# ViT layer on one core: narrower stationary operands in the attention scores, and the maximum of the last three steps subtracted on VectorE

## The chip, the cores and the metric

The kernel runs on one core of a Trainium2 chip. The metric is the device time of one execution in microseconds. A core has TensorE (PE, matmuls out of SBUF into PSUM), VectorE (DVE), ScalarE (ACT), GpSimd (POOL, which here works on SBUF alone) and SyncE (SP, which issues the DMAs). Each engine runs its own list of instructions in order, and the lists meet at semaphores.

## The reference

One vision-transformer layer on 16 images of 96x96x3. Patches of 16x16 give 36 tokens per image and a width of 192:

```
h = patchify(x) @ W + b                                  # 16 x 36 x 192
q, k, v = split(h @ w_qkv.T)                             # 12 heads of 64
q = q * rsqrt(norm(q over heads) + eps); k likewise
scores = softmax(q @ k.T / scale[head])                  # per image and head: 36 x 36
h = layernorm(h + (scores @ v) @ w_out.T + b_out)
h = layernorm(h + ffn(h))                                # 8 experts, the best 2 per token
```

The FFN is a clamped gated one with sigmoid GELU. All data are fp32.

## The kernel before, in words

The 16 images are taken two at a time, in NU = 8 attention steps u = 0 to 7. The two images of a step, 36 tokens each, lie in PSUM lanes 0 to 35 and 64 to 99, so that LANES = 100. The 12 heads lie side by side, 36 columns each, six in one bank and six in the next. A step's bank pair is `s_bank(u) = 2 * (u % 2)`.

What a step u consists of, with the engine that does it:

- `scores(u)` (TensorE, L1488): 24 matmuls of q against k, in quarters of the array (64 rows by 64 columns), shown as 48 records since the data are fp32. The moving operand has 36 columns. The stationary one has 36 columns for the second image and 64 for the first; the 28 lanes more give lanes 36 to 63 defined values.
- `row_max(u)` (VectorE, L1020): the negated maximum of each row and head.
- `subtract_max(u)` (TensorE, L1500): two matmuls of a 100x100 identity against the broadcast maxima, which add the negated maximum to the scores in PSUM.
- `exps(u)` (ScalarE, L721): exponential from PSUM into the probabilities buffer u % 3 in SBUF.
- `row_sum(u)` and `row_recip(u)` (VectorE, L1027, L1034), then `probs(u)` (GpSimd, L525), which multiplies by the reciprocals.
- `p_transpose(u)` (TensorE, L1513), `pt_evac(u)` (ScalarE), `weighted(u)` (TensorE, L1530, probabilities times v, in quarters of the array too), `o_evac(u)` (ScalarE).

`project(g)` (TensorE, L1547 and L1550) multiplies a tile of about 108 tokens by the output weights and adds the residual, in one PSUM bank that all g share. Then the first layer norm: `ln1_stats(g)` (VectorE, L1039 to L1043, three instructions), `root(g)` (GpSimd, L531), `ln1(g)` (VectorE, L1057 and L1059). `project(g + 1)` waits for `ln1(g)`, since it writes the same bank. `h1_transpose(g)` (TensorE, L1559) and the router's `logits(g)` follow. From about 70 us on the experts' matmuls fill TensorE.

The order on each engine is written out by hand. TensorE, for k = 2 to 6: subtract_max(k), scores(k+1), weighted(k-2), p_transpose(k-1), with half of a v projection at k = 2, 3 and project(k-4) at k = 4, 5. Then subtract_max(7), h1_transpose(0), project(2), h1_transpose(1), weighted(5), p_transpose(6), logits(0), logits(1), h1_transpose(2).

VectorE, for k = 2 to 7: ln1_stats(k-5) at k = 5, 6; row_sum(k); ln1(0) at k = 5; row_max(k+1); ln1(1) at k = 6; row_recip(k); q_norm(k+3) at k = 2, 3, 4 (L976, the query's norm of a later step).

GpSimd, for k = 0 to 7: root(1) at k = 6; w_lo(7), w_lo(9), w_lo(10) at k = 3, 5, 6 (the low parts of later weights, L482, or L460 and L467); probs(k); at k = 4 then w_lo(8) and root(0); k_norm(k+3) (L518) while there is one. The low parts of q, k and weight data exist because large matmuls are made of several fp32r ones.

Waits that matter: `exps(u)` waits for subtract_max(u) and for p_transpose(u-3), which frees the probabilities buffer; `scores(u)` waits for exps(u-2), which frees the bank pair, and for the norms; `h1_transpose(0)` and `(1)` wait for exps(6) and exps(7), whose banks they write.

Of the kernel before, what the change touches and what calls it, by code (L numbers as in the profile page):

```python
# [10 lines left out]
B, SEQ = 16, 36  # L11
# [3 lines left out]
NP = H // 2  # L15
# [3 lines left out]
NU = B // 2  # L19
ST = 2 * SEQ  # L20
FST = 2 * ST
LANES = 64 + SEQ
# [13 lines left out]
def head_of(b, i, r):  # L36

    return 4 * i + (2 * r if b == 0 else 3 - 2 * r)
# [10 lines left out]
LAST_LO = 2 * NT - 1  # L49
NACT = 6  # L50
IN_PSUM = 3
XW = T + 2 * 128
STG = 6
NAT = 3
# [5 lines left out]
def vit_layer(nc, xw_in, w_qkv_a, w_qkv_b, w_out, w_gu_a, w_gu_b, w_down, small, out):  # L60
    f32, f32r, bf16, u32 = mybir.dt.float32, mybir.dt.float32r, mybir.dt.bfloat16, mybir.dt.uint32
    ALU = mybir.AluOpType
    ACT = mybir.ActivationFunctionType
# [3 lines left out]
    with ctx:  # L67
        def sb(name, shape, dt=f32):
            return ctx.enter_context(nc.sbuf_tensor(name, shape, dt))
# [4 lines left out]
        def f(ap):  # L74
            return ap.bitcast(f32)
# [7 lines left out]
        reg_r = sb("reg_r", [128, 4608 + 2 * NACT * TM + 3 * T], f32r)  # L83
        xw = reg_r[:, 0:NC * 2 * XW].rearrange("p (c k n) -> p c k n", c=NC, k=2)
        wd = reg_r[:, 0:NT * 384].rearrange("p (c n) -> p c n", c=NT)
# [4 lines left out]
        stage = sb("stage", [128, STG, STGW])  # L90
        reg_x = sb("reg_x", [128, NC * XW])
        xs = reg_x[:, :].rearrange("p (c n) -> p c n", c=NC)
# [4 lines left out]
        qk = reg_q[:, :].rearrange("p (m n) -> p m n", m=2 * NP)  # L97
# [45 lines left out]
        mx_r = sb("mx_r", [128, 2, H], f32r)  # L143
# [21 lines left out]
        ps = ctx.enter_context(nc.psum_tensor("ps", [128, 8, BANK], f32))  # L165
# [7 lines left out]
        def probabilities(u):  # L173

            return (Pr[:, 0], Pr[:, 1], Pr2)[u % 3]

        def slots_of(u, rows):

            return probabilities(u)[rows, :].rearrange("p (h j) -> p h j", h=H)[:, :, 0:SEQ]
# [93 lines left out]
        def lo_done(k):  # L273

            return (s_wlod, k + 1) if k < 2 else (s_wlop, w_count(k))
# [28 lines left out]
        def s_bank(u):  # L304
            return 2 * (u % 2)
# [9 lines left out]
        def spread_count(n):  # L315

            return (32 if n % 3 == 2 else 16) * (2 if n >= NT + IN_PSUM else 1)

# [28 lines left out]
        def pair_of(n):  # L347
            return pair(place(n))
# [7 lines left out]
        def gate_of(n):  # L356

            w = TS[n // NT]
            return ps[:, pair_of(n)[0], 0:w] if n >= IN_PSUM else glu[:, n, 0:w]

        def up_of(n):

            w = TS[n // NT]
            return ps[:, pair_of(n)[1], 0:w] if n >= IN_PSUM else upw[:, n, 0:w]

# [14 lines left out]
        def _(sp):  # L380
            sp.dma_start(xs[:, 0, 0:WX + TH], xw_in[0, :, 0:WX + TH]).then_inc(s_x[0], 16)
            sp.dma_start(xs[:, 0, WX + TH:XW], xw_in[0, :, WX + TH:XW]).then_inc(s_xb, 16)
            for c in range(1, NC):
# [21 lines left out]
            def spread(b):  # L405
# [4 lines left out]
                else:  # L410
                    sp.wait_ge(*lo_done(16))
                    for c in range(IN_PSUM, NT):
                        sp.wait_ge(s_spr[c], spread_count(c))
# [170 lines left out]
        def _(act):  # L584
# [130 lines left out]
            def exps(u):  # L715

                act.wait_ge(s_sub, u + 1)
                if u >= 3:
                    act.wait_ge(s_pt, u - 2)
                b = s_bank(u)  # L720
                nc.scalar.activation(slots_of(u, slice(0, LANES)).rearrange("p (b h) j -> p b h j", b=2),  # L721
                                     ps[0:LANES, b:b + 2, 0:6 * SEQ].rearrange("p b (h j) -> p b h j", h=6),
                                     ACT.Exp).then_inc(s_e, 1)
# [181 lines left out]
        def _(dve):  # L905
# [108 lines left out]
            def row_max(u):  # L1014

                dve.wait_ge(s_s, u + 1)
                if u >= 2:
                    dve.wait_ge(s_e, u - 1)
                b = s_bank(u)
                nc.vector.reduce_max(mx_r[0:LANES, u % 2, :].rearrange("p (b h) -> p b h", b=2),  # L1020
                                     ps[0:LANES, b:b + 2, 0:6 * SEQ].rearrange("p b (h j) -> p b h j", h=6),
                                     X, negate=True).then_inc(s_mx, 1)

            def row_sum(u):

                dve.wait_ge(s_e, u + 1)
                nc.vector.reduce_sum(psum_e[0:LANES, u % 2, :], slots_of(u, slice(0, LANES)), X).then_inc(s_sum, 1)  # L1027

            def row_recip(u):

                dve.wait_ge(s_sum, u + 1)
                if u >= 2:
                    dve.wait_ge(s_p, u - 1)
                nc.vector.reciprocal(rinv[0:LANES, u % 2, :], psum_e[0:LANES, u % 2, :]).then_inc(s_rinv, 1)  # L1034
# [10 lines left out]
            def ln1_stats(g):  # L1045
                n = TSIZES[g]
                dve.wait_ge(s_op, g + 1)
                if g >= 1:
                    dve.wait_ge(s_h1, 2 * g)
                statistics(g, ps[0:n, L_BANK, 0:D], s_st, s_mv, s_ve)  # L1050

            def ln1(g):
                n = TSIZES[g]
                dve.wait_ge(s_rstd, g + 1)
                if g >= 2:
                    dve.wait_ge(s_ht, g - 1)
                nc.vector.tensor_scalar(h1[0:n, g % 2, 0:D], ps[0:n, L_BANK, 0:D], mv[0:n, 0:1], rstd[0:n, 0:1],  # L1057
                                        ALU.subtract, ALU.mult).then_inc(s_h1, 1)
                nc.vector.tensor_scalar(h1[0:n, g % 2, D:D + DB], ps[0:n, L_BANK, DA:D], mv[0:n, 0:1], rstd[0:n, 0:1],  # L1059
                                        ALU.subtract, ALU.mult).then_inc(s_h1, 1)  # L1060
# [79 lines left out]
            def weigh(n):  # L1140

                a, c = divmod(n, NT)
                if n < IN_PSUM:
                    dve.wait_ge(s_bm, n + 1)
# [10 lines left out]
            def copy_iota():  # L1155

                dve.wait_ge(s_b, IN_PSUM)
                nc.vector.tensor_copy(ps[:, B_BANK, IOTA_COL:IOTA_COL + 8], sm[:, C_IOTA:C_IOTA + 8]).then_inc(s_iota, 1)
# [74 lines left out]
            q_norm(2)  # L1233
            row_max(1)
            row_sum(0)
            row_recip(0)
            q_norm(3)
# [5 lines left out]
            for k in range(2, NU):  # L1243
                if k in (5, 6):
                    ln1_stats(k - 5)
                row_sum(k)
                if k == 5:
                    ln1(0)
                if k + 1 < NU:
                    row_max(k + 1)  # L1250
                if k == 6:
                    ln1(1)
                row_recip(k)
                if k in (2, 3, 4):
                    q_norm(k + 3)
# [71 lines left out]
        def _(pe):  # L1327
# [142 lines left out]
            def scores(u):  # L1470

                o, bank = ST * u, s_bank(u)
                if u == 0:
                    pe.wait_ge(s_kn0, 1)
                if u < 2:
                    pe.wait_ge(s_vev, u + 1)
                else:
                    pe.wait_ge(s_e, u - 1)
                pe.wait_ge(s_qn, u + 1)
                if u:  # L1480
                    pe.wait_ge(s_kn, u)
                for i in range(3):
                    for r in range(2):
                        for b, img in ((0, 0), (1, 1), (0, 1), (1, 0)):
                            m = head_of(b, i, r) // 2
                            rows, c, t = slice(64 * b, 64 * b + 64), SEQ * (2 * i + r), o + SEQ * img
                            n = (64, SEQ)[img]
                            last = mm(ps[64 * img:64 * img + n, bank + b, c:c + SEQ], qk[rows, m, t:t + n],  # L1488
                                      qk[rows, NP + m, t:t + SEQ], start=(i == 0 and r == 0), stop=False,
                                      skip_group_check=True)  # L1490
                last.then_inc(s_s, 1)

            def subtract_max(u):

                bank = s_bank(u)
                if u == 0:
                    pe.wait_ge(s_const, 1)
                pe.wait_ge(s_mx, u + 1)
                for b in range(2):
                    last = mm(ps[0:LANES, bank + b, 0:6 * SEQ].rearrange("p (h j) -> p h j", h=6), ident_r[0:LANES, 0:LANES],  # L1500
                              mx_r[0:LANES, u % 2, 6 * b:6 * b + 6].unsqueeze(2).to_broadcast([LANES, 6, SEQ]),
                              start=False, stop=True, skip_group_check=True)
                last.then_inc(s_sub, 1)
# [177 lines left out]
            v_proj(3, (1,))  # L1681
            p_transpose(0)
            for k in range(2, NU - 1):
                subtract_max(k)
                scores(k + 1)
                weighted(k - 2)
                p_transpose(k - 1)
                if k in (2, 3):
                    v_proj(4, (k - 2,))
                if k in (4, 5):  # L1690
                    project(k - 4)
            subtract_max(7)
            h1_transpose(0)
            project(2)
            h1_transpose(1)
# [111 lines left out]
```

## Time and profile before

| | |
|---|---|
| median of 3 runs | 136.16 us (135.83 to 136.19) |
| the profiled execution | 136.0 us, span 134.2 us |
| PE busy | 127.7 us (95%) |
| DVE busy | 95.5 us (71%) |
| ACT busy | 81.3 us (61%) |
| POOL busy | 74.7 us (56%) |
| attention steps | about 38 to 73 us |

The span is the time from the first to the last instruction that the profiler saw. Matmuls are pipelined and their ends are modelled, so a short wait of TensorE does not show as idle time: the distance between starts has to be read instead. A row of a timeline gives start, duration, engine, line, operation and operands, and in brackets the idle time before it and what ended it.

### The profile page before, as it was taken

What the parts mean: (1) busy time and instruction counts of PE and PEld (TensorE: products, weight loads), DVE (VectorE), ACT (ScalarE), POOL (GpSimd) and SP (SyncE); (2) the same over time, 40 slices, a digit from 0 to 9 for tenths busy, and PEclk for the clock granted to TensorE, in tenths of its full rate; (3) what the DMA queues carried; (4) which work ended last, traced back from release to release, by engine and by line L of the source; (5) the groups of instructions that cost most, each with busy time, mean ns of one, the idle gap of its engine ahead of it and who ended that gap; (6) DMA issues with size and microseconds to landing.
All of it is one profiled execution on the core that took longest, in us unless ns stands there. A gap on an engine that the chain in (4) does not pass through costs nothing. (4 is left out here: it accounts for less than half of the span.)

```text
span 134.2 us, 3973 instructions
## 1 busy us (share of the span) xinstructions
PE 127.7 (95%) x1564; PEld 119.3 (89%) x1565; DVE 95.5 (71%) x240; ACT 81.3 (61%) x168; POOL 74.7 (56%) x83
## 2 busy tenths in 40 slices
PE   6999999999999999999999999999999999999960
PEld 2778999999899999999989999999899999999950
DVE  0009689927967969567677688898987776788862
ACT  3028689998865258487759673655354446333771
POOL 7300428953078999998760482689853442344600
PEclk9999999999999999999999999999999999999996
DMA  4899974550022222522393047600006650000022
GB/s 129 272 384 405 412 265 158 154 210 0 5 66 56 66 57 70 150 70 76 89 330 126 0 94 171 164 26 0 0 0 156 146 144 20 5 2 0 2 67 65
DMA packets 8987, 15.47 MB, mean 115 GB/s; under 512 B 1224, under 2 KB 5896, under 8 KB 8968
## 3 DMA queue, kind: packets, MB, share of 16 engines
q1 hardware_dynamic: 8968, 15.22, 36.5%
q8 instruction: 12, 0.20, 0.6%
q14 instruction: 7, 0.06, 0.1%
HBM read 9.96 MB, written 0.44 MB: 78 GB/s over the span
## 5 line engine op out<-in xcount | busy, mean ns | idle before, releaser
L542 POOL TENSOR_TENSOR reg_r<-reg_p,reg_r 128x324 fp32r<-128x324 f32 (+1 forms) x23 | 18.7, 811 | 19.2 <-ACT reg_r L793 19.1
L482 POOL TENSOR_TENSOR reg_w<-stage,reg_w 128x768 fp32r<-128x768 f32 x12 | 22.3, 1867 | 10.9 <-DVE w L1121 6.3
L793 ACT ACTIVATE reg_r<-reg_p 128x324 fp32r<-128x324 f32 (+1 forms) x23 | 10.2, 444 | 13.5 <-DVE reg_p L1172 13.4
L1377 PE MATMUL ps<-reg_r,reg_w 128*128 128x324 f32 (+1 forms) x48 | 15.0, 312 | 0.0
L784 ACT ACTIVATE ps<-ps,sm 128x252 f32<-128x252 f32 (+1 forms) x21 | 9.7, 464 | 8.7 <-PE ps L1381 8.5
L1380 PE MATMUL ps<-reg_r,reg_w 128*128 128x324 f32 (+1 forms) x48 | 14.2, 296 | 0.0
L1378 PE MATMUL ps<-reg_r,reg_w 128*128 128x324 f32 (+1 forms) x48 | 14.2, 295 | 0.0
L1381 PE MATMUL ps<-reg_r,reg_w 128*128 128x324 f32 (+1 forms) x48 | 14.1, 295 | 0.0
L1379 PE MATMUL ps<-reg_r,reg_w 128*128 128x324 f32 (+1 forms) x48 | 14.1, 294 | 0.0
L1137 DVE TENSOR_SCALAR ps<-ps,bup 128x252 f32<-128x252 f32 (+1 forms) x21 | 10.8, 513 | 3.3 <-PE ps L1381 3.2
L518 POOL TENSOR_TENSOR reg_q<-reg_q,rnorm 128x432 f32<-128x432 f32 x7 | 8.9, 1275 | 6.4 <-ACT rnorm L679 6.4
L1172 DVE SCALAR_TENSOR_TENSOR reg_p<-ps,reg_q 128x252 f32<-128x252 f32 (+1 forms) x21 | 9.5, 453 | 2.3 <-DVE reg_q L1152 0.5
L601 ACT ACTIVATE reg_w<-stage 128x768 fp32r<-128x768 f32 x13 | 10.9, 841 | 0.1
L1550 PE MATMUL ps<-wout,reg_q 128*108 128x192 f32 (+2 forms) x60 | 10.6, 326 | 0.0
L1377 PEld LDWEIGHTS ps<-reg_r,reg_w 128*128 128x128 f32 x48 | 9.1, 189 | 0.7 <-DVE reg_p L1172 0.3
L1550 PEld LDWEIGHTS ps<-wout,reg_q 128*108 128x108 f32 (+2 forms) x60 | 9.6, 179 | 0.0
L1381 PEld LDWEIGHTS ps<-reg_r,reg_w 128*128 128x128 f32 x48 | 9.1, 189 | 0.0
L1379 PEld LDWEIGHTS ps<-reg_r,reg_w 128*128 128x128 f32 x48 | 9.1, 189 | 0.0
L1378 PEld LDWEIGHTS ps<-reg_r,reg_w 128*128 128x128 f32 x48 | 9.1, 189 | 0.0
L1380 PEld LDWEIGHTS ps<-reg_r,reg_w 128*128 128x128 f32 x48 | 9.0, 188 | 0.0
L1488 PEld LDWEIGHTS ps<-reg_q 64*64 64x64 f32 (+1 forms) x384 | 6.4, 122 | 1.1 <-issue 0.4
L1488 PE MATMUL ps<-reg_q 64*64 64x36 f32 (+1 forms) x384 | 7.2, 215 | 0.0
(206 smaller groups left out, 391.2 us busy)
## 6 DMA issues: line engine op xcount, KB each, us to landing
reg_x<-xw_in SPq DMA_DIRECT2D x5, 416.0 KB, 6.6
stage<-w_gu_a SPq DMA_DIRECT2D x4, 384.0 KB, 3.6
stage<-w_gu_b SPq DMA_DIRECT2D x4, 384.0 KB, 4.0
reg_r<-reg_x SPq DMA_DIRECT2D x24, 54.0 KB
stage<-w_qkv_a SPq DMA_DIRECT2D x3, 384.0 KB, 8.1
stage<-w_qkv_b SPq DMA_DIRECT2D x3, 384.0 KB, 8.0
stage<-w_down SPq DMA_DIRECT2D x3, 384.0 KB, 3.8
stage<-wrow SPq DMA_DIRECT2D x8, 126.0 KB, 2.4
```

What stands on the lines that cost most here:

```text
L482: nc.gpsimd.tensor_tensor(dst[:, 1, :], raw, f(dst[:, 0, :]), ALU.subtract).then_inc(s_wlop, 1)
L542: nc.gpsimd.tensor_tensor(acts[:, n % NACT, 1, 0:w], act_f[:, n % 4, 0:w], f(acts[:, n % NACT, 0, 0:w]), ALU.subtract).then_inc(s_alo, 1)
L601: nc.scalar.activation(dst, raw, ACT.Copy).then_inc(s_whi, 1)
L793: nc.scalar.activation(acts[:, n % NACT, 0, 0:w], act_f[:, n % 4, 0:w], ACT.Copy).then_inc(s_ahi, 1)
L1137: nc.vector.tensor_scalar(up_of(n), ps[:, pair_of(n)[1], 0:TS[n // NT]], bup1[:, c:c + 1], LIMIT + 1, ALU.add, ALU.min).then_inc(s_u, 1)
L1377: mm(out_ap, w_a(0), x[:, 0, cols], start=True, stop=False)
L1378: mm(out_ap, w_a(1), x[:, 0, cols], start=False, stop=False)
L1379: mm(out_ap, w_a(0), x[:, 2, cols], start=False, stop=False)
L1380: mm(out_ap, w_b(0), x[:, 1, cols], start=False, stop=False)
L1381: return mm(out_ap, w_b(1), x[:, 1, cols], start=False, stop=True)
L1488: last = mm(ps[64 * img:64 * img + n, bank + b, c:c + SEQ], qk[rows, m, t:t + n], qk[rows, NP + m, t:t + SEQ], start=(i == 0 and r == 0), ...
L1550: last = mm(ps[0:n, L_BANK, 0:D], o_stationary(g, m), wout[:, m, :], start=False, stop=(m == NP - 1), skip_group_check=True)
```

## The change

- `scores(u)` for u of 2 and above uses 36 stationary columns for the first image as well. Lanes 36 to 63 of a bank then keep what an earlier step left there.
- For u = 5, 6, 7 the two matmuls of subtract_max are gone from TensorE. VectorE gets its own `subtract_max(u)`: one tensor_tensor that adds the negated maxima to the scores in PSUM and writes the result into the probabilities buffer in SBUF. It waits for row_max(u) and for p_transpose(u-3), and stands directly behind row_max(k+1) in VectorE's list.
- `exps(u)` for those steps works in place in the SBUF buffer.

```diff
+SUB_DVE = 5
...
+                if u >= SUB_DVE:
+                    nc.scalar.activation(slots_of(u, slice(0, LANES)), slots_of(u, slice(0, LANES)), ACT.Exp).then_inc(s_e, 1)
+                    return
...
+            def subtract_max(u):
+
+                dve.wait_ge(s_mx, u + 1)
+                dve.wait_ge(s_pt, u - 2)
+                b = s_bank(u)
+                nc.vector.tensor_tensor(slots_of(u, slice(0, LANES)).rearrange("p (b h) j -> p b h j", b=2),
+                                        ps[0:LANES, b:b + 2, 0:6 * SEQ].rearrange("p b (h j) -> p b h j", h=6),
+                                        f(mx_r[0:LANES, u % 2, :]).rearrange("p (b h) -> p b h", b=2).unsqueeze(3)
+                                        .to_broadcast([LANES, 2, 6, SEQ]), ALU.add).then_inc(s_sub, 1)
...
                 if k + 1 < NU:
                     row_max(k + 1)
+                if SUB_DVE <= k + 1 < NU:
+                    subtract_max(k + 1)
                 if k == 6:
                     ln1(1)
                 row_recip(k)
...
-                            n = (64, SEQ)[img]
+                            n = 64 if img == 0 and u < 2 else SEQ
                             last = mm(ps[64 * img:64 * img + n, bank + b, c:c + SEQ], qk[rows, m, t:t + n],
-                                      qk[rows, NP + m, t:t + SEQ], start=(i == 0 and r == 0), stop=False,
+                                      qk[rows, NP + m, t:t + SEQ], start=(i == 0 and r == 0),
+                                      stop=(u >= SUB_DVE and i == 2 and r == 1),
                                       skip_group_check=True)
...
             for k in range(2, NU - 1):
-                subtract_max(k)
+                if k < SUB_DVE:
+                    subtract_max(k)
                 scores(k + 1)
...
-            subtract_max(7)
             h1_transpose(0)
```

## Rows read from the trace of the kernel before

**Rows 1.** Busy time by stretch: us, length, each engine's busy time, clock, DMA.

```profile
54.00:64.00 10.00, 9.95 (x245) 9.35 (x244) 6.09 (x19) 6.69 (x12) 9.29 (x10) 1.00 0.34 101
...
130.00:132.00 2.00, 0.04 (x1) 0.00 (x0) 1.72 (x6) 0.93 (x4) 0.00 (x0) 0.90 0.21 61
132.00:134.20 2.20, 0.00 (x0) 0.00 (x0) 0.00 (x0) 0.00 (x0) 0.00 (x0) 0.50 0.31 88
```

**Rows 2.** Timeline of TensorE, 53 to 69 us: start, duration, line, operands.

```profile
53.49 0.72 PE L1513 MATMUL ps<-pairs,reg_p 100*100 100x100 f32 x6
54.05 0.38 PE L1547 MATMUL ps<-ident,hb 128*108 128x128 f32 x2
...
56.09 0.49 PE L1500 MATMUL ps<-mx_r,ident_r 100*100 100x216 f32 x2
56.51 0.83 PE L1488 MATMUL ps<-reg_q 64*64 64x36 f32 x45
...
58.04 0.72 PE L1513 MATMUL ps<-pairs,reg_p 100*100 100x100 f32 x6
58.82 0.40 PE L1547 MATMUL ps<-ident,hb 128*108 128x128 f32 x2
...
60.87 0.49 PE L1500 MATMUL ps<-mx_r,ident_r 100*100 100x216 f32 x2
...
63.86 0.40 PE L1547 MATMUL ps<-ident,hb 128*108 128x128 f32 x2
...
68.47 0.32 PE L1559 MATMUL ps<-ident,reg_h 108*128 108x108 f32 x1
```

**Rows 3.** Timeline of GpSimd, 50 to 63 us.

```profile
51.85 0.91 POOL L525 TENSOR_TENSOR reg_p<-reg_p,rinv 100x432 f32<-100x432 f32 x1
52.72 1.47 POOL L518 TENSOR_TENSOR reg_q<-reg_q,rnorm 128x432 f32<-128x432 f32 x1
54.47 1.15 POOL L525 TENSOR_TENSOR reg_p<-reg_p,rinv 100x432 f32<-100x432 f32 x1 [0.28 <-DVE rinv L1034]
55.58 1.82 POOL L482 TENSOR_TENSOR reg_w<-stage,reg_w 128x768 fp32r<-128x768 f32 x1
57.35 0.56 POOL L531 TENSOR_TENSOR rstd<-var_e,half 108x1 f32<-108x1 f32 x1
57.87 1.11 POOL L518 TENSOR_TENSOR reg_q<-reg_q,rnorm 128x432 f32<-128x432 f32 x1
...
62.06 0.56 POOL L531 TENSOR_TENSOR rstd<-var_e,half 108x1 f32<-108x1 f32 x1 [0.43 <-DVE var_e L1043]
```

**Rows 4.** Timeline of VectorE, 50 to 64 us.

```profile
50.73 2.50 DVE L976 TENSOR_TENSOR reg_q<-reg_q,rnorm 128x432 f32<-128x432 f32 x1
...
53.66 0.59 DVE L1020 TENSOR_REDUCE mx_r<-ps 100x12 fp32r<-100x432 f32 x1
54.18 0.21 DVE L1034 RECIPROCAL rinv<-psum_e 100x12 f32<-100x12 f32 x1
54.31 0.54 DVE L976 TENSOR_TENSOR reg_q<-reg_q,rnorm 128x432 f32<-128x432 f32 x1
56.42 0.37 DVE L1039 BATCH_NORM_STATS2 stats<-ps 108x6 f32<-108x192 f32 x1 [1.57 <-PE ps L1550]
...
57.95 0.48 DVE L1057 TENSOR_SCALAR reg_h<-ps,mv,rstd 108x192 f32<-108x192 f32 x1 [0.17 <-POOL rstd L531]
58.34 0.33 DVE L1059 TENSOR_SCALAR reg_h<-ps,mv,rstd 108x64 f32<-108x64 f32 x1
...
62.48 0.60 DVE L1020 TENSOR_REDUCE mx_r<-ps 100x12 fp32r<-100x432 f32 x1
62.99 0.47 DVE L1057 TENSOR_SCALAR reg_h<-ps,mv,rstd 108x192 f32<-108x192 f32 x1
```

**Rows 5.** Weight loads of scores by shape, 38 to 76 us: count, busy us, mean ns.

```profile
L1488 PEld LDWEIGHTS ps<-reg_q 64*64 64x64 f32 x192 | 6.4, 134 | 1.1 <-issue 0.4
...
L1488 PEld LDWEIGHTS ps<-reg_q 64*36 64x36 f32 x192 | 5.0, 109 | 0.0
```

## Prediction

> **What bounds the kernel now.** I began with the busy time by stretches. Between 54 and 64 us TensorE is busy 9.95 of 10 us, which looks as if every matmul taken away were time won. GpSimd is busy 9.29 of the same 10 us [rows 1]. So two engines look full, and busy shares cannot say which one sets the pace. I therefore read the timelines of TensorE, GpSimd and VectorE side by side.
>
> TensorE's timeline [rows 2] has, in each step, scores and weighted (56.51 to 58.04), p_transpose (58.04), then project. After p_transpose(3) at 53.49 and before project there is 0.56 us, and after p_transpose(4) at 58.04 there is 0.78 us for the same six instructions. So project(1) at 58.82 waited about 0.25 us. It waits for ln1(0), whose second VectorE instruction ends at 58.34 + 0.33 = 58.67 [rows 4]. project(2) at 63.86 waits for ln1(1) in the same way: its first part starts at 62.99, and by the pattern of ln1(0) its second ends 0.72 us later, at 63.71. The modelled ends of the matmuls hide both waits in the busy time.
>
> Where does ln1(0) come from? It starts at 57.95, when the GpSimd instruction root(0) (57.35, 0.56) has ended at 57.91 [rows 3, 4]. root(0) itself had its input early: ln1_stats(0) began at 56.42. It started at 57.35 because w_lo(8) (55.58, 1.82) held GpSimd until 57.40. w_lo(8) follows probs(4) (54.47, 1.15). And probs(4) is the one GpSimd instruction here with idle time before it, 0.28 us, ended by VectorE's row_recip(4) (54.18, 0.21, so done at 54.39). VectorE has no idle time noted from q_norm(6) at 50.73 to row_recip(4). So the path that sets the end runs through VectorE up to row_recip(4), GpSimd (probs(4), w_lo(8), root(0)), VectorE (ln1(0)), TensorE (project(1)), VectorE (ln1_stats(1), row_sum(6), row_max(7), ln1(1)), TensorE (project(2)), and then ln1(2) up to h1_transpose(2) at 68.47 [rows 2]. From there on TensorE works without a gap of note until the tail.
>
> **Part 1: 36 stationary columns in scores(2) to scores(7).** Half the weight loads of a scores step shrink from 64 to 36 columns. In the trace a 64-column load takes 134 ns and a 36-column load 109 ns [rows 5]. Per step, 12 loads follow one another in each 64-column quarter of the array, so the estimate is 12 x 25 ns = 0.30 us of TensorE time per step, and the bounds are 0 and 0.30. The kernel already has 36-column loads in the other quarters. The 96 matmul records from 56.51 to 58.04 are 16 ns apart [rows 2], so issue is not slower than that.
>
> The Trainium skill ("TensorE: Matmul & The Clock Gate", section "Back-to-back issue gap") gives about 60 cycles, 25 ns, for any matmul of 1 to 64 moving columns. By it the width of the stationary operand could not matter here and this part would save nothing. The trace disagrees with it already, at 16 ns.
>
> Four of the six steps (scores 2 to 5) lie before project(0): up to 1.2 us. But p_transpose(3), at 53.49, needs probs(3), which GpSimd finishes at 51.85 + 0.91 = 52.76 [rows 3]. So p_transpose(3) and project(0) gain at most 0.7 us. Nothing of it reaches project(1): root(0) is held by GpSimd's own queue, not by project(0).
>
> **Part 2: subtract_max(5), (6), (7) leave TensorE.** From subtract to the scores behind it it takes 0.42 us (56.09 to 56.51, and the next at 60.87 is the same pair) [rows 2]. So at most 0.42 each, 1.26 in all, and nothing at the least. The first lies before scores(6), in the stretch in which TensorE will wait for ln1(0) anyway. The second lies after project(1), but scores(7) is not what VectorE waits for there, as shown below. The third, in the k = 7 part, lies in front of h1_transpose(0) and project(2), which wait for ln1(1). So all three are worth nothing on the path.
>
> **Part 3: the subtraction on VectorE.** One instruction more per step, 100x432 from PSUM to SBUF. Nearest rows: row_max, 100x432 from PSUM, starts at 53.66 and the next starts at 54.18, 0.52 us later (0.60 us long); q_norm(7), 128x432 with two SBUF inputs, takes 0.54 [rows 4]. The subtraction waits for row_max to finish, so it cannot overlap its end. I take 0.60 to the end of row_max, 0.04 to start, and 0.52 until the next may start, less the 0.52 that row_max had already: 0.64 us more in the queue. Bounds: 0.54 from below, and from above 0.60 + 1.96 if the instruction can be blocked as q_norm(6) was (2.50 us against 0.54, beside GpSimd's work). I take no blocking: q_norm reads two SBUF tensors, while ln1(0), which reads PSUM as this one does, ran 0.48 us at 57.95 beside k_norm(7) at 57.87 [rows 3, 4].
>
> What is queued behind it, step by step:
>
> subtract_max(5) comes before row_recip(4). That is the one instruction that GpSimd waited for. GpSimd was free at 54.19 (52.72 + 1.47), so no slack is left over: probs(4), w_lo(8), root(0), ln1(0) and project(1) all go 0.64 us later, to 59.46.
>
> subtract_max(6) comes before row_recip(5). probs(5) waits behind w_lo(9) for long after it. Nothing.
>
> subtract_max(7) comes between row_max(7) and ln1(1). ln1_stats(1) follows project(1), so it is 0.64 late. Then VectorE works without idle time up to row_max(7) (62.48 before) and ln1(1) (62.99 before). root(1), 62.06 + 0.56 = 62.62, is done before ln1(1) can start and stays so. Another 0.64 us go straight into ln1(1), project(2) and h1_transpose(2).
>
> The exponential in place costs ScalarE about the same as from PSUM. exp(6) no longer waits for project(1), and its row_sum stands behind ln1_stats(1) anyway. exp(7) follows the subtraction, which by the same steps runs from 63.76 (62.48 + 0.64 + 0.64) to 64.36. h1_transpose(1) needs it only behind project(2), so after 67. Nothing.
>
> **The sum.** 136.0 us of the profiled execution (span 134.2 and 1.8 around it) + 0.64 + 0.64 = 137.3. The median of the runs, 136.16, is 0.16 above the profiled one: 137.4 us.
>
> **Rivals.**
>
> *TensorE sets the pace.* Then all that leaves it is won: 6 x 0.30 + 3 x 0.42 = 3.06 us, so 133.1 us. For it: 9.95 of 10 us busy. Against it: 0.25 us of waiting at project(1), and the two chains that end there. It would decide only if GpSimd's chain from 50 us on were earlier by itself. Chance 0.09.
>
> *One of the two charges is dodged.* q_norm(6) asked for 0.54 us of work and held VectorE for 2.50 us beside GpSimd's w_lo(7) and probs(3). Two shortened scores steps lie before exp(3), for which VectorE waits ahead of it, so q_norm(6) comes 0.3 to 0.6 us earlier, at 50.1 to 50.4. If q_norm(6) then gets in before GpSimd's long instructions, VectorE is ahead by more than a microsecond, row_recip(4) is in time even with the subtraction before it, and probs(4) even wins its 0.28 us. Left: 0.64 - 0.28 = 0.36, so 136.5 us. For it: the same instruction took 0.54 us elsewhere. Against: w_lo(7) ended at 51.85 and, at the 1.82 us of w_lo(8), began near 50.03, still before it. Chance 0.16.
>
> *TensorE's clock falls.* In the new order TensorE is through with p_transpose(4) by about 57.2 (56.09 - 0.7 + 1.25 + 0.5) and waits until 59.46 for project(1): 2.2 us without a matmul; some 1.5 us follow before project(2). In the trace the granted clock is full in all stretches with work, and its mean is 0.90 from 130 to 132 and 0.50 (1.2 GHz) after 132 [rows 1]. That puts the fall at 131.6, some 1.8 us after the last matmuls of the window before. If it falls here too, project(1) takes twice its 2.05 us (58.82 to 60.87), and that is on the path: 137.4 + 2.1 = 139.5 us. Against it: full work before and after the pause. Chance 0.12. The Trainium skill ("TensorE: Matmul & The Clock Gate", section "HAM oscillation — how this bites in real kernels") states that pauses between bursts of matmuls can bring the clock to half; the end of this trace shows such a fall, no stretch inside the kernel does.
>
> **How the numbers follow.** The forecast has 0.63, with its own range 136.9 to 138.0 (subtraction 0.54 to 0.75 in the queue, twice, and the spread of runs). The range for 8 in 10 goes from the dodged charge to near the clock case: 136.2 to 138.8. What a measurement of this kernel can tell from no change is about 0.3%, 0.4 us: up to 136.57 counts as the same. The dodged charge, 136.5, is half "same" and half slower with its spread. Faster 0.10, same 0.12, slower 0.78.
>
> **What would show each step.** Right: TensorE idle for about 2 us before project(1), ending with ln1(0); the new VectorE instruction at 0.5 to 0.6 us between row_max(5) and row_recip(4); probs(4), w_lo(8), root(0) each some 0.6 us later; ln1(1) some 1.3 us later, with the rest of the kernel shifted alike. Scores followed by weighted in 1.25 us in place of 1.53. Wrong: project(1) at or before 58.8; q_norm(6) much shorter than 2.5 us; a subtraction over 1 us long; a granted clock below full between 57 and 66 us.

## The result and the profile after

The changed kernel takes 137.61 us (median of 4 runs, 137.13 to 141.18) against 136.18 us (135.83 to 136.49) before: ratio 1.0084, 95% interval 1.0046 to 1.0123. Run again on another chip beside the experiments: 137.47 against 136.18 us, ratio 1.0097 (1.0049 to 1.0144). It is slower by about 1%, as forecast (137.4). Some runs are several microseconds longer, before and after alike; the medians given here and below count them, the ratios leave the longest out.

The profiled execution took 137.13 us, span 135.3. TensorE's timeline (start, duration) answers to [rows 2]; lines are those of the changed file, where p_transpose is L1530, scores L1504, weighted L1547, project L1564 and L1567, h1_transpose L1576.

```profile
49.77 0.38 PE L1530 MATMUL ps<-pairs,Pr 100*100 100x100 f32 x2
51.12 0.50 PE L1530 MATMUL ps<-pairs,Pr 100*100 100x100 f32 x4 [0.97 <-issue]
...
56.76 0.65 PE L1504 MATMUL ps<-reg_q 64*36 64x36 f32 x48
57.25 0.91 PE L1547 MATMUL ps<-reg_p,reg_r 36*64 36x36 f32 x48
58.09 0.72 PE L1530 MATMUL ps<-pairs,reg_p 100*100 100x100 f32 x6
59.79 0.40 PE L1564 MATMUL ps<-ident,hb 128*108 128x128 f32 x2 [0.98 <-DVE reg_h L1073]
...
65.39 0.40 PE L1564 MATMUL ps<-ident,hb 128*108 128x128 f32 x2 [1.09 <-DVE reg_h L1073]
...
70.00 0.31 PE L1576 MATMUL ps<-ident,reg_h 108*128 108x108 f32 x1
```

TensorE now stands idle before project(1) and project(2), each time until ln1 (L1073) is done. Both waits were in the kernel before too, hidden under modelled ends; now the profile notes them. What shows it is the distance from the end of the second ln1 instruction to project: 0.15 us before (58.67 to 58.82) and 0.15 us in the changed kernel's second profile (59.40 to 59.55). GpSimd, to compare with [rows 3] (probs(4), w_lo(8), root(0)):

```profile
55.44 1.15 POOL L526 TENSOR_TENSOR reg_p<-reg_p,rinv 100x432 f32<-100x432 f32 x1 [1.29 <-DVE rinv L1048]
56.55 1.81 POOL L483 TENSOR_TENSOR reg_w<-stage,reg_w 128x768 fp32r<-128x768 f32 x1
58.33 0.55 POOL L532 TENSOR_TENSOR rstd<-var_e,half 108x1 f32<-108x1 f32 x1
```

VectorE, to compare with [rows 4]. L1041 is row_sum, L1024 row_max, L1033 the new subtraction, L1048 row_recip, L1071 ln1:

```profile
50.47 2.71 DVE L980 TENSOR_TENSOR reg_q<-reg_q,rnorm 128x432 f32<-128x432 f32 x1
53.47 0.60 DVE L1041 TENSOR_REDUCE psum_e<-reg_p 100x12 f32<-100x432 f32 x1 [0.29 <-ACT reg_p L725]
53.99 0.60 DVE L1024 TENSOR_REDUCE mx_r<-ps 100x12 fp32r<-100x432 f32 x1
54.62 0.61 DVE L1033 TENSOR_TENSOR Pr<-ps,mx_r 100x432 f32<-100x432 f32 x1
55.15 0.22 DVE L1048 RECIPROCAL rinv<-psum_e 100x12 f32<-100x12 f32 x1
...
63.37 0.60 DVE L1024 TENSOR_REDUCE mx_r<-ps 100x12 fp32r<-100x432 f32 x1
64.00 0.61 DVE L1033 TENSOR_TENSOR reg_p<-ps,mx_r 100x432 f32<-100x432 f32 x1
64.53 0.47 DVE L1071 TENSOR_SCALAR reg_h<-ps,mv,rstd 108x192 f32<-108x192 f32 x1
```

From row_max(5) to row_recip(4) it is now 1.16 us, 0.52 before; from row_max(7) to ln1(1) 1.16, 0.51 before. That is 0.64 and 0.65 us more, the two charges. GpSimd waited 1.29 us for row_recip(4) in place of 0.28.

One thing in these rows was not foreseen: TensorE stopped for about a microsecond within p_transpose(2), at 50.15, and exp(4), row_sum(4) and row_recip(4) came some 0.36 us later for it. So part of GpSimd's 1.29 us is the stall: without it the wait is 0.91 us. In the second profile of the same kernel (e8_changed_again) p_transpose(2) is 0.96 us long in place of 0.72, no idle time is noted in it, and row_sum(4) does not wait. These are its rows:

```profile
57.31 0.72 PE L1530 MATMUL ps<-pairs,reg_p 100*100 100x100 f32 x6
59.55 0.40 PE L1564 MATMUL ps<-ident,hb 128*108 128x128 f32 x2 [1.52 <-DVE reg_h L1073]
...
65.16 0.40 PE L1564 MATMUL ps<-ident,hb 128*108 128x128 f32 x2 [1.10 <-DVE reg_h L1073]
```

### The profile page after: what moved, and what is told of

It is laid out like the page before. It is cut to its first block and busy times, and to the rows that moved or that the text cites. A ratio compares the mean times of both kernels' runs of the same rounds, so it can differ in the third digit from the quotient of the medians.

```text
span 135.3 us, 3968 instructions
## 1 busy us (share of the span) xinstructions
PE 126.1 (93%) x1559; PEld 117.0 (86%) x1559; DVE 97.4 (72%) x243; ACT 81.3 (60%) x168; POOL 74.5 (55%) x83
## 5 line engine op out<-in xcount | busy, mean ns | idle before, releaser
L1567 PE MATMUL ps<-wout,reg_q 128*108 128x192 f32 (+2 forms) x60 | 10.6, 326 | 0.0
L1567 PEld LDWEIGHTS ps<-wout,reg_q 128*108 128x108 f32 (+2 forms) x60 | 9.6, 179 | 0.0
L739 ACT ACTIVATE reg_q<-ps 128x432 f32<-128x432 f32 x8 | 4.2, 531 | 5.9 <-PE ps L1547 5.9
L980 DVE TENSOR_TENSOR reg_q<-reg_q,rnorm 128x432 f32<-128x432 f32 x8 | 7.6, 955 | 0.0
```

Of the source, the lines that this page charges most:

```text
L1567: last = mm(ps[0:n, L_BANK, 0:D], o_stationary(g, m), wout[:, m, :], start=False, stop=(m == NP - 1), skip_group_check=True)
```

## The experiments

Each was run in five rounds beside the kernel before: e1 to e4 on one chip, e5 to e8 on a second, e9 and e10 on a third. Ratios are to the kernel before on the same chip. A profile's clock starts at its own first instruction, so in the table all starts are counted from that of scores(0), up to which all kernels are the same (38.08 to 38.98 us into the span). Four steps of the path, each from one profile:

| kernel | row_recip(4) | project(1) | project(2) | h1_transpose(2) | ratio (95%) |
|---|---|---|---|---|---|
| before | 15.61 | 20.25 | 25.29 | 29.90 | 1 |
| changed, first profile | 16.60 | 21.24 | 26.84 | 31.45 | 1.0084 (1.0046 to 1.0123) |
| changed, e8_changed_again | 16.24 | 20.88 | 26.49 | 31.09 | 1.0097 (1.0049 to 1.0144) |
| e1_columns_only | 16.17 | 20.85 | 25.89 | 30.50 | 0.9951 (0.9911 to 0.9990) |
| e2_vector_only | 16.24 | 20.88 | 26.49 | 31.09 | 1.0076 (1.0036 to 1.0117) |
| e3_subtract_late | 15.59 | 20.80 | 25.76 | 30.39 | 1.0016 (0.9978 to 1.0055) |
| e4_only_third_early | 15.60 | 20.81 | 28.10 | 32.71 | 1.0082 (1.0048 to 1.0115) |
| e5_subtract_last | 15.59 | 20.23 | 25.20 | 29.82 | 0.9982 (0.9952 to 1.0011) |
| e9_only_fifth_early | 16.24 | 20.89 | 25.85 | 30.48 | 1.0087 (1.0054 to 1.0120) |
| e10_only_seventh_early | 15.59 | 20.24 | 25.85 | 30.45 | 1.0038 (1.0015 to 1.0062) |
| e6_root_first | 15.69 | 20.42 | 25.46 | 30.06 | 0.9939 (0.9908 to 0.9969) |
| e7_last_and_root_first | 15.60 | 19.75 | 24.71 | 29.33 | 0.9961 (0.9919 to 1.0002) |

**Which part costs.** e1_columns_only is the kernel before with this one edit:

```diff
-                            n = (64, SEQ)[img]
+                            n = 64 if img == 0 and u < 2 else SEQ
```

> The kernel before with one part of the change: 36 stationary columns for the first image from u = 2 on; the maximum is still subtracted by TensorE in all steps. My theory (the path runs through VectorE up to row_recip(4), then GpSimd, ln1(0), project(1), ln1(1), project(2)): a scores step and its weighted take 1.25 us in place of 1.53, but project(1) starts at 58.8 us as before and the time is that of the kernel before, 136.2 us within 0.4. Rival 'TensorE sets the pace': 6 x 0.28 = 1.7 us faster, 134.5. Second rival (the narrower columns themselves cost something, by the 1 us stall inside p_transpose(2) near 50 us that the changed kernel shows): the stall is here too, row_sum(4) waits for exp(4), and project(1) is 0.3 us late: 136.5.

Measured: 135.70 against 136.53 us. TensorE as the bound, 134.5 us, is refuted. "No change" is not borne out either: the columns alone are faster by 0.1 to 0.9%, an interval that only just leaves out 1. Its profile shows the stall of TensorE again, 1.16 us, and project(1) 0.6 us late from it, as the second rival said for this profile; it is one of the longer runs (136.49 us, which is also the rival's time), so the rival does not describe the median.

e2_vector_only is the changed kernel with `n = (64, SEQ)[img]` back.

> The changed kernel with the 64 stationary columns back in all steps: the other part alone, the subtraction of steps 5 to 7 on VectorE. My theory: the whole loss is here. Subtraction 0.6 us ahead of row_recip(4) and again ahead of ln1(1): project(1) 0.63 us later than before, project(2) 1.27 later, time 137.2 to 137.5 us, without the stall near 50 us. Rival (the loss comes from the stall or from the columns): 136.2 to 136.6.

Measured: 137.74 us, over the expected 137.2 to 137.5; the clock fell in this profile after the steps of the table (last section). All the loss is here, and its four steps in the table are those of e8_changed_again to the hundredth: with the subtraction early on VectorE, narrower columns move nothing on the path.

**Where the subtraction stands.** e3_subtract_late:

```diff
-                if SUB_DVE <= k + 1 < NU:
-                    subtract_max(k + 1)
                 if k == 6:
                     ln1(1)
                 row_recip(k)
+                if SUB_DVE <= k + 1 < NU:
+                    subtract_max(k + 1)
```

> The changed kernel with VectorE's subtraction moved behind row_recip(k), and so at k = 6 also behind ln1(1). Every instruction is the same, only VectorE's order differs. My theory: both charges are gone, project(1) starts at 58.8 (59.1 if the stall near 50 us stays), ln1(1) at 63.0 to 63.3, time 136.0 to 136.5. Rival (the extra work on VectorE or the wait of exp(5) to (7) on VectorE costs as such, wherever it stands): 137.3 or more.

Measured: 136.97 us, between the two expectations (its profiled run 136.32). row_recip(4) was in time, yet project(1) was not. GpSimd's probs(4), and VectorE's row_recip(4), subtraction and q_norm(7), of this kernel:

```profile
54.63 1.72 POOL L526 TENSOR_TENSOR reg_p<-reg_p,rinv 100x432 f32<-100x432 f32 x1 [0.27 <-DVE rinv L1048]
```

```profile
54.34 0.21 DVE L1048 RECIPROCAL rinv<-psum_e 100x12 f32<-100x12 f32 x1
54.48 0.59 DVE L1033 TENSOR_TENSOR Pr<-ps,mx_r 100x432 f32<-100x432 f32 x1
54.98 0.60 DVE L980 TENSOR_TENSOR reg_q<-reg_q,rnorm 128x432 f32<-128x432 f32 x1
```

In the kernel before q_norm(7) started 0.16 us ahead of probs(4), which took 1.15 us. Here it started 0.35 us into probs(4), which took 1.72. A VectorE instruction in another place moved one behind it onto GpSimd's, and 0.57 of the 0.64 us came back. In e4_only_third_early, which has the same order at this place, probs(4) took 1.71 us. e4_only_third_early has (7) ahead of ln1(1) and the rest late:

> As the kernel with the late subtraction, but subtract_max(7) stands ahead of ln1(1) again, as in the changed kernel. It tells whether the two charges add. My theory: project(1) as with the late subtraction, ln1(1) and project(2) 0.64 us later than there, and so is the whole: 136.7 to 137.1. Rival (the second subtraction lies beside root(1) on GpSimd and is hidden): the same time as with the late subtraction, all of the loss belonging to subtract_max(5).

Measured: 137.96 us, over both expectations. Its profile can't answer the question, since TensorE's clock fell in it (last section). It fell in other runs too: 7 of the 11 have a mean granted clock of 0.984 or less, and the four others took 136.82 to 137.31 us, near the theory's 136.7 to 137.1. So I put the subtraction last. e5_subtract_last:

```diff
                 row_recip(k)
                 if k in (2, 3, 4):
                     q_norm(k + 3)
+                if SUB_DVE <= k + 1 < NU:
+                    subtract_max(k + 1)
```

> As the kernel with the late subtraction (behind row_recip(k)), but at k = 4 it stands behind q_norm(7) too. There q_norm(7) asked for SBUF in the middle of probs(4), and probs(4) took 1.72 us instead of 1.15, which gave the charge back. Theory (the place beside GpSimd's instruction decides): row_recip(4), q_norm(7), probs(4) fall as in the kernel before, probs(4) takes 1.15 us, project(1) starts at 58.8, and the time is that of the kernel with the columns alone, 135.6 to 136.1 us. Rival (any 0.6 us more of work on VectorE in this stretch lengthens GpSimd's probs(4) or w_lo(8), wherever it stands): probs(4) or w_lo(8) some 0.5 us longer and 136.6 to 137.0 us as with the late subtraction.

Measured: 135.72 us, as the theory said. Its probs(4), then its project(1) and project(2):

```profile
54.13 1.15 POOL L526 TENSOR_TENSOR reg_p<-reg_p,rinv 100x432 f32<-100x432 f32 x1 [0.27 <-DVE rinv L1048]
```

```profile
58.48 0.40 PE L1564 MATMUL ps<-ident,hb 128*108 128x128 f32 x2 [0.50 <-DVE reg_h L1073]
...
63.45 0.40 PE L1564 MATMUL ps<-ident,hb 128*108 128x128 f32 x2 [0.43 <-DVE reg_h L1073]
```

With the same instructions on every engine as in the changed kernel, the loss is gone (0.9982 against 1.0097 on the same chip), so it belongs to VectorE's order. TensorE still waits for ln1 at both places, which is why the matmuls taken from it bring nothing.

**The two charges by themselves.** e9_only_fifth_early is e5 with `subtract_max(5)` ahead of row_recip(4); e10_only_seventh_early is e5 with `subtract_max(7)` ahead of ln1(1).

> As the kernel with the subtraction last, but subtract_max(5) stands ahead of row_recip(4) as in the changed kernel; (6) and (7) stay last. It measures the first charge alone. My theory: row_recip(4), probs(4), w_lo(8), root(0) and project(1) 0.64 us later than with the subtraction last, and so the whole: 136.3 to 136.6 us. Rival (this first delay is taken up before project(2), by ln1(1) waiting for row_max(7) anyway): 135.7, as with the subtraction last.

> As the kernel with the subtraction last, but subtract_max(7) stands ahead of ln1(1) as in the changed kernel; (5) and (6) stay last. It measures the second charge alone, free of the collision of q_norm(7) with probs(4). My theory: project(1) as with the subtraction last, ln1(1) and project(2) 0.64 us later, the whole 136.3 to 136.6 us; with the first charge's 0.64 the two add to the changed kernel's distance from the kernel with the subtraction last. Rival (hidden beside root(1) on GpSimd): 135.7.

Measured: 137.16 and 136.46 us, against 135.89 for the kernel before beside them. By the table, h1_transpose(2) is at 29.82 with neither, at 30.48 with the fifth (+0.66), at 30.45 with the seventh (+0.63), and at 31.09 with both (+1.27): they add. They still do at the end of the kernel: from scores(0) to the last instruction the profiles have 95.15 us with neither, 95.82 with the fifth, 95.82 with the seventh and 96.43 with both (span less the start of scores(0)). The runs do not show it as sharply. 0.64 us is 0.47% of the time. By the differences to e5's ratio (0.9982), the fifth costs 1.05% (1.0087), the seventh 0.56% (1.0038) and both 1.15% (1.0097), each ratio being uncertain by 0.2 to 0.5%. The two alone would sum to 1.61%, over the 1.15% of both. The order of sizes is borne out; that the charges are alike and add rests on one profile each.

**What holds project(1).** e6_root_first is e1 with GpSimd's list at k = 4 changed; e7_last_and_root_first is e5 with the same edit:

```diff
-                if k == 4:
-                    w_lo(8)
-                    root(0, TSIZES[0], s_ve, s_rstd)
                 if k + 3 < NU:
                     k_norm(k + 3)
+                if k == 4:
+                    root(0, TSIZES[0], s_ve, s_rstd)
+                    w_lo(8)
```

> The kernel with the columns alone (subtraction on TensorE), and GpSimd's order at k = 4 changed: k_norm(7), root(0), w_lo(8) in place of w_lo(8), root(0), k_norm(7). My theory says that w_lo(8), 1.82 us long, holds root(0), and root(0) holds project(1), while TensorE is early thanks to the columns. So root(0) starts at about 56.7 to 57.2, project(1) at 58.0 to 58.3 in place of 58.8, and all behind it moves alike: 0.6 us faster than with the columns alone, 135.0 to 135.3 us. Rival (GpSimd does not bound here; TensorE or the DMAs do): no change against the columns alone, 135.7.

> Both parts of the change, with the subtraction last in VectorE's list of the step and GpSimd's root(0) ahead of w_lo(8). It tells whether the subtraction on VectorE is worth anything once neither queue pays for it. Theory: TensorE waits at project(1) and project(2) in any case, so the 3 x 0.25 to 0.42 us taken from it stay unused: 135.0 to 135.4 us, the same as with the subtraction on TensorE. Rival: TensorE is now the bound and the subtraction's leaving gives 0.5 us or more: 134.5 or less.

Measured: 135.32 and 136.11 us, against 136.18. e6_root_first is faster than both the kernel before and the changed one (ratio 0.9939). Its own profile does not show the early project(1) that was expected: TensorE stalled for 0.63 us in p_transpose(2), project(0) came late, and root(0) waited 0.76 us for ln1_stats(0). Against e1_columns_only (0.9951, on another chip) the difference is not resolved. The profiles of e5 and e7 differ in this edit alone: project(1) is 0.48 us earlier (19.75 against 20.23) and h1_transpose(2) 0.49. GpSimd's root(0), of e5 and then of e7:

```profile
57.02 0.56 POOL L532 TENSOR_TENSOR rstd<-var_e,half 108x1 f32<-108x1 f32 x1
```

```profile
56.56 0.56 POOL L532 TENSOR_TENSOR rstd<-var_e,half 108x1 f32<-108x1 f32 x1 [0.18 <-DVE var_e L1057]
```

It follows w_lo(8) without idle time in e5 and waits only for its input in e7. So w_lo(8) did hold root(0), and that holds project(1). What the subtraction's leaving TensorE adds there (e7 against e6) is not resolved in the runs, whose intervals overlap. e7's 136.11 us lies over both of its expectations; 4 of its 12 runs have a mean granted clock of 0.987 or less, the profiled one among them.

**The changed kernel again.**

> The changed kernel as it is, again, beside the others and in more runs. My theory: 137.2 to 137.7 us, 0.6 to 1.1% over the kernel before. Of interest in its profile: whether the 1 us stall of TensorE inside p_transpose(2) is there again (it was with the columns alone, and not in the two kernels with the subtraction moved, whose TensorE program is the same). If it is there, row_sum(4) waits for exp(4) and project(1) starts near 59.8; if it isn't, project(1) starts at 59.4 and ln1(1) 1.27 us later than before.

Measured: 137.47 us, and without the stall project(1) at 20.88, 0.63 us after that of the kernel before. The ten runs fall into two groups. Five have a mean granted clock of 0.996 to 1.0 and took 136.42 to 136.96 us; five have 0.975 to 0.981 and took 137.99 to 139.69. Of the kernel before beside them 4 of 33 runs have a clock of 0.987 or less, and the 29 others have a median of 136.07. So among these runs the change costs 0.67 us (136.74 against 136.07), about 0.5%, where the clock holds, and the rest of the 1% comes with TensorE's clock falling more often. On the first chip three runs with the full clock took 137.13 to 137.71 us, and the profiled one of them had the stall, so the split is that of these ten runs.

## Why the prediction was right, step by step

*The path.* Right: VectorE to row_recip(4), GpSimd to root(0), ln1(0), project(1), and again to project(2). e5 and e7 show it by moving it from two sides.

*Part 1.* Right in sign, somewhat too large. From scores to p_transpose it is 1.33 us (56.76 to 58.09) in place of 1.53, so 0.20 us is saved and not 0.30. Why not the whole of 12 times 25 ns wasn't tried. That it would be worth nothing on the path holds for the changed kernel (e2 equals e8). For the kernel before it doesn't hold in the runs: e1 is 0.5% faster. No profile shows a step of the path that is earlier for it (its own had the stall, 0.60 us at project(1), and is 0.56 us longer from scores(0) to the end), so where that gain lies stays open.

*Part 2.* Right: nothing. TensorE waits 1.52 and 1.10 us at the two projects in e8.

*Part 3.* Right in mechanism and size. The instruction took 0.61 us and cost 0.64 us in the queue, with the terms of the forecast: it starts 0.63 us after row_max, and the next instruction 0.53 us after it, where the next one followed row_max by 0.52 before. subtract_max(7), which runs beside w_lo(10) on GpSimd, was not blocked; for subtract_max(5) GpSimd stood idle. Forecast +0.64 at project(1) and +1.28 at h1_transpose(2); e8 has +0.63 and +1.19, since the path up to there is 0.08 us shorter in e5 than before.

*From h1_transpose(2) to the end.* Wrong: the sum took both 0.64 through to the end whole. On TensorE e8 is 1.29 us behind the kernel before at 88 us into the span and 0.93 behind at 95. VectorE's shift falls from 1.29 to 0.93 at one instruction, ahead of TensorE's. It is the fourth expert's last VectorE instruction, here of the kernel before and then of e8:

```profile
86.58 0.50 DVE L1172 SCALAR_TENSOR_TENSOR reg_p<-ps,reg_q 128x324 f32<-128x324 f32 x1 [0.46 <-DVE reg_q L1152]
```

```profile
87.51 0.50 DVE L1186 SCALAR_TENSOR_TENSOR reg_p<-ps,reg_q 128x324 f32<-128x324 f32 x1
```

Before, VectorE stood still for 0.46 us with its own instruction as the only releaser found; in e8 only 0.10 us passes at this place (87.41 to 87.51). The 0.46 is in all profiles of kernels with VectorE's old list (before, e1, e6) and in none of the nine with three instructions more. So the kernels with the subtraction on VectorE stand still 0.36 us less here, wherever in the list it is. Why VectorE stands still is open; the count of instructions ahead is one thing in which these kernels differ, and no run tells it from the rest of the change.

*The total.* Near the forecast in part by luck. From scores(0) to the last instruction it is 95.63 us before and 96.43 in e8: 0.80 us more, where the sum had 1.28. Two things that the sum did not have lift the runs towards 137.4: the stall of TensorE in the first profile (96.75 us, 1.12 more), and the fallen clock in half of the runs of e8.

*The rivals.* "TensorE sets the pace" is refuted by e1 and e5. "One charge is dodged" did not happen: q_norm(6) took 2.71 us. "The clock falls" was given 0.12. It did not happen in the first three runs, at 137.13 to 137.71 us with a mean granted clock of 0.999 or more, but by the clocks of the runs in half of e8's. The chance was too low for a kernel that waits so long at project(1).

## What to carry to other kernels

Work taken from an engine that looks 95% busy brings nothing if that engine waits at a later point for a chain through others; read the distance between starts at each join, and find the instruction with idle time before it, since that is where one more instruction costs its whole length. When work is moved onto another engine's list, put it behind whatever another engine waits for, and look at what it pushes back: here 0.6 us of work cost 0.64 us at one place, 0.57 by a collision at the next, and nothing at the third.

## What the runs showed of the hardware that was not expected

**TensorE's clock can fall inside the kernel, and did so more often where TensorE has the longest wait.** Busy times by stretch, granted clock in the third column from the right, of e4_only_third_early, and its project(1) and the scores behind it:

```profile
54.00:59.00 5.00, 3.42 (x111) 2.93 (x109) 3.11 (x10) 3.37 (x6) 4.88 (x4) 1.00 0.38 121
59.00:63.00 4.00, 3.96 (x14) 3.54 (x15) 1.05 (x3) 1.75 (x3) 2.84 (x3) 0.57 0.29 82
```

```profile
59.04 0.44 PE L1566 MATMUL ps<-ident,hb 128*108 128x128 f32 x2 [1.62 <-DVE reg_h L1073]
59.28 3.79 PE L1569 MATMUL ps<-wout,reg_q 128*108 128x192 f32 x12
63.00 0.65 PE L1506 MATMUL ps<-reg_q 64*36 64x36 f32 x48
```

The stretch from 59 to 63 us was granted 0.57 on average, for the most part 1.2 GHz, right after a pause of some 1.8 us (1.62 by the modelled ends). project(1) took 3.96 us in place of 2.05. e8 has much the same pause before project(1), 1.52 us by the modelled ends, and no fall. Two other profiles (e2, e7) have a fall later, at 71.0 and at 69.1 us, of about the same length: in each of the three the mean over the stretch corresponds to 3.4 us at 1.2 GHz. There TensorE had worked without a pause of note for 6 us, since the start of project(2) at 64.97 and 62.99, so a pause directly ahead is not what these two share with e4.

The mean clock of a run tells of falls without a profile: the nine profiles without one have 0.989 to 1.000, the three with one 0.980 and 0.985. Of the runs of the four kernels whose row has 1.4 us or more of idle time before project(1) (e3, e4, e8, e9), 21 of 39 have a mean of 0.988 or less; of all other runs beside them, 31 of 152. So a longer wait of TensorE goes with more falls, and a wait can have a price beyond its length, in some executions. What decides about a single execution is not shown. The Trainium skill ("TensorE: Matmul & The Clock Gate", section "HAM oscillation — how this bites in real kernels") warns that pauses between bursts of matmuls can bring the clock to half; this trace agrees, with 0.57 granted in the stretch behind the pause; e2's and e7's falls, behind 6 us of work, are not of that kind.

**TensorE stopped for 0.35 to 1.16 us inside p_transpose(2)** in four of the ten profiles with narrow columns (the changed kernel once of twice, e1, e5, e6), with "issue" as the reason, and noted in neither of those with 64 columns (before, e2). Two profiles of the same program differ in it. Smaller stops show as a longer p_transpose(2), 0.93 to 0.96 us in place of 0.72 in e3, e7, e8 and e9, and 0.85 in e2, which has 64 columns. The stop costs up to 0.6 us at project(1) (e1). What TensorE waits for is not in the profile's rows.

**q_norm, a VectorE instruction with two SBUF inputs, and GpSimd's instructions take longer by where they meet.** q_norm(7) took 0.54 us when it started just ahead of probs(4), and that took 1.15 us; when it started inside probs(4) it took 0.60 and probs(4) 1.72; q_norm(6), which starts inside w_lo(7), took 2.50 to 2.74 us itself. The subtraction, with one input in PSUM, took 0.54 to 0.61 us in every place. That the number of SBUF inputs is what makes the difference was not tried by itself.
